# A macaron block on one core: router logits made with the router stationary, the first and last pass's gates spread by TensorE, small weights turned on chip, and every engine's order written anew

## The reference

```
x = x + 0.5 * ffn(layernorm(x))
x = x + attn(layernorm(x))          # 16 heads of 16, each token sees 64 keys back
x = x + 0.5 * ffn(layernorm(x))

ffn(X):  shared = silu(X @ sW1 + sb1) @ sW2 + sb2
         logits = X @ routing_W.T + expert_bias            # 8 experts
         g      = sqrt(softplus(logits)), only the two largest kept
         return shared + sum_e g[:, e] * (silu(X @ rW1[e] + rb1[e]) @ rW2[e] + rb2[e])
```

## Time and profile before

| what | value |
|---|---|
| median of three runs | 1589.93 us |
| profiled execution | 1584.86 us |
| its span | 1583.1 us |
| TensorE busy | 1479.5 us, 93% of the span |
| VectorE, ScalarE, GpSimd busy | 1179.6, 1128.6, 779.8 us |
| mean granted TensorE clock | 0.973 |

### The profile page before, as it was taken

One profiled execution on the slowest core, in us unless ns is written; L12 is line 12 of the kernel. 1 busy time (PEld: TensorE's weight loads), 2 busy tenths in 40 slices (PEclk: granted clock), 3 DMA queues, 4 the chain that ended last, 5 costly groups with the idle time before them and its releaser, 6 DMA issues.

```text
span 1583.1 us, 40702 instructions
## 1 busy us (share of the span) xinstructions
PE 1479.5 (93%) x13632; PEld 1333.7 (84%) x13632; DVE 1179.6 (75%) x4771; ACT 1128.6 (71%) x3400; POOL 779.8 (49%) x789
## 2 busy tenths in 40 slices
PE   2888999999999999999999999999999999998967
PEld 1777889898898989899898989989898988987756
DVE  5747677878878787887878787787878788675643
ACT  3358686877878687777878677787868778766823
POOL 2334454645555454555455455555546455453423
PEclk9899999999999999999999999999999999999888
DMA  4253635444453634445463543547364453625202
GB/s 116 64 164 106 174 111 177 121 125 137 122 172 95 192 110 138 129 124 161 121 181 102 155 128 116 157 124 180 95 176 121 126 138 107 173 82 161 82 20 67
DMA packets 269957, 203.86 MB, mean 129 GB/s; under 512 B 154379, under 2 KB 224421, under 8 KB 269749
## 3 DMA queue, kind: packets, MB, share of 16 engines
q1 hardware_dynamic: 266308, 201.17, 44.1%
q10 hardware_dynamic: 3408, 0.02, 0.1%
q0 software_dynamic: 32, 0.07, 0.0%
HBM read 146.06 MB, written 42.47 MB: 119 GB/s over the span
## 4 chain that ended last, share of the span: by engine, by line
PE 85%; DVE 5%; issue 3%; SPq 2%; DMA 2%; POOL 1%; ACT 1%; ACTq 0%; POOLq 0%; DVEq 0%
PE gb L937 12%; PE gb L939 11%; PE gb L938 11%; PE yb L937 9%; PE yb L939 8%; PE yb L938 8%; PE ptb L1000 7%; PE sb_ L991 6%; PE cxb L1019 4%; PE gb L1029 2%; PE gb L1041 2%; PE gb L1039 2%; PE gb L947 1%; SPq L479 1%; PE yb L1073 1%
## 5 line engine op out<-in xcount | busy, mean ns | idle before, releaser
L563 POOL TENSOR_TENSOR gl<-ag,gh 128x512 fp32r<-128x512 f32 x288 | 379.9, 1320 | 240.3 <-ACT gh L661 239.7
L546 POOL TENSOR_TENSOR pr<-pr,rinv 128x512 f32<-128x512 f32 x256 | 272.2, 1064 | 300.2 <-DVE rinv L822 298.3
L617 ACT ACTIVATE pr<-pr,mx 128x128 f32<-128x128 f32 x1024 | 397.5, 395 | 9.7 <-DVE mx L814 7.0
L937 PE MATMUL yb<-w2h,gh 128*128 128x256 f32 x1152 | 336.8, 292 | 12.4 <-POOL gl L563 12.3
L938 PE MATMUL yb<-w2h,gl 128*128 128x256 f32 x1152 | 324.0, 281 | 0.0
L939 PE MATMUL yb<-w2l,gh 128*128 128x256 f32 x1152 | 324.0, 281 | 0.0
L669 ACT ACTIVATE tt<-gb,b1half 128x512 f32<-128x512 f32 x288 | 195.4, 683 | 153.3 <-PE gb L939 147.7
L814 DVE CUSTOM_DVE_ANT_0 pr<-sb_,mask 128x128 f32<-128x128 f32 x1024 | 235.2, 285 | 53.8 <-issue 34.5
L881 DVE SCALAR_TENSOR_TENSOR ag<-gb,b,gate 128x512 f32<-128x512 f32 x256 | 188.2, 744 | 83.0 <-ACT tt L669 63.2
L661 ACT ACTIVATE gh<-ag 128x512 fp32r<-128x512 f32 x288 | 180.7, 628 | 95.1 <-DVE ag L887 66.8
L937 PE MATMUL gb<-xh,w1h 128*128 128x512 f32 x576 | 243.4, 423 | 2.6 <-DVE ag L881 2.0
(11 more groups left out here) (138 smaller groups left out, 2730.9 us busy)
## 6 DMA issues: line engine op xcount, KB each, us to landing
gate<-gates_pair SPq DMA_DIRECT2D x256, 256.0 KB, 3.7
ks<-qk_dram SPq DMA_DIRECT2D x256, 128.0 KB, 3.0
qs<-qk_dram SPq DMA_DIRECT2D x512, 64.0 KB, 2.6
qk_dram<-qkh SPq DMA_DIRECT2D x64, 256.0 KB, 2.4
qk_dram<-qkl SPq DMA_DIRECT2D x64, 256.0 KB, 2.7
vb<-va SPq DMA_DIRECT2D x32, 384.0 KB, 5.8
xres<-L_attn_x_dram SPq DMA_DIRECT2D x16, 512.0 KB, 4.1
out_dram<-xres SPq DMA_DIRECT2D x16, 512.0 KB, 4.0
```

Of the source, the lines that this page charges most:

```text
L546: nc.gpsimd.tensor_tensor(pr[:, k], pr[:, k], rinv[:, k, :].unsqueeze(2).to_broadcast([P, NP, P]), ALU.mult).then_inc(a_pn, 1)
L563: nc.gpsimd.tensor_tensor(gl[:, k, :], ag[:, k, :], gh[:, k, :].bitcast(F32), ALU.subtract).then_inc(f_gl, 1)
L617: nc.scalar.activation(pr[:, k, r, :], pr[:, k, r, :], ACT.Exp, bias=mx[:, k, r:r + 1], scale=-1.0, accum_out=rsum[:, k, r:r + 1]).then_in ...
L937: nc.tensor.matmul(dst, ah, bh, start=start, stop=False, **kw)
```

## The change

1. **Logits.** L now loads the router once for each half of the features (`rw`, widened with zeros to 128 columns) and streams `xh` and `xl`, 512 columns each: 4 matmuls. The result is turned: experts on partitions, rows 0 to 7 from the router's high part and rows 8 to 15 from its low part. A new ScalarE step lt copies the 128 by 512 tile to `lgt` in SBUF. A new TensorE step M takes each of its four 128-token parts as the stationary operand and a matrix `fold` of ones and zeros (8 columns) as the moving one, in true fp32, which turns the logits back and adds the two parts. Lr loses one of its two additions. The new value waits in the same bank, which is therefore held from L until Lr has read M's result.
2. **Gates of p0 and q15** (`by_pe`). They no longer go through DRAM. TensorE step B takes a column of the selection matrix `sel` as a broadcast stationary operand and streams `cft`: every partition gets the gate of one expert, in `sb_` or `ptb` in turn. ScalarE step K copies it to `gate`. So 16 matmuls of 512 columns and 16 copies are new, and two G1 and 16 sp are gone, as are two cr.
3. **Small weights.** The router and the biases were read transposed, element by element. Now their rows are read as they lie and TensorE step Wt turns them. GpSimd makes `sel`, `fold` and the zeros of `rw`.
4. **Loads** stand in the order of their use: x0, then 1s, 1r, 2s, 2r, then x1. The expert weights are split in halves (1r and 1t, 2r and 2t), so that their high and low parts are made in pieces. The zeroing Wz of `qs` and `va` moves from VectorE to GpSimd.
5. **All tables** are new. HEAD and TAIL of TensorE now reach further into the steady state, and ORDER, the steady period itself, is another sequence.

```diff
-P6-5 qC-6 S9-5 pY7-4 P7-5 S10-5 pY8-4 qH1-6 S11-5 qH2-6 U7-5 qY0-6 pX0-3 pX1-3 P8-5 qH3-6 P9-5 qY1-6 qH4-6
+aX0-2 qY1-4 aX1-2 qY2-4 S13-3 qH5-4 Q00-2 qY3-4 Q01-2 qY4-4 S14-3 pX0-1 pX1-1 qH6-4 S15-3 Q10-2 pL-1 P13-3
...
-pX0=0 pX1=0 pL=0 pH0=0 pC=0 pY0=0 pH1=0 pH2=0 pH3=0 pH4=0 pH5=0 pY1=0 pH6=0 pY2=0 pH7=0 pY3=0 pH8=0 pY4=0
+Wt=0 pX0=0 pX1=0 pL=0 pH0=0 pH1=0 pM=0 pH2=0 pC=0 pB0=0 pB1=0 pB2=0 pB3=0 pH3=0 pB4=0 pB5=0 pY0=0 pH4=0
...
-        rw = sb("rw", [P, KC, 2 * E], F32R)
-        rwf = sb("rwf", [P, KC, E])
+        rw = sb("rw", [P, KC, P], F32R)
+        fold = sb("fold", [P, E])
...
+        by_pe = {("p", 0), ("q", B - 1)}
...
+            apart_ |= {(x + k, b) for x, b in by_pe for k in ["G1", "cr"] + ["sp%d" % m for m in range(E)]}
...
-            for c in range(KC):
-                act.dma_start(rwf[:, c, :], routing_w[:, c * P:(c + 1) * P].rearrange("e p -> p e"),
-                              allow_slow_non_contiguous=True).then_inc(w_in[0], 16)
+            act.dma_start(small[0:E, 0:KC * P], routing_w).then_inc(w_small, 16)
+            act.dma_start(small[0:1, KC * P:], sb1.rearrange("(a p) -> a p", a=1)).then_inc(w_small, 16)
+            act.dma_start(small[1:NE, KC * P:], rb1).then_inc(w_small, 16)
...
+                elif s[1:] == "lt":
+                    n = nth(s, b)
+                    act.wait_ge(f_lgt, n + 1)
+                    nc.scalar.activation(lgt, bank(s[0] + "L", b), ACT.Copy).then_inc(f_lgs, 1)
...
+                elif s[1] == "K":
+                    n, m = nth(s, b), int(s[2])
+                    act.wait_ge(f_gpe, E * (s[0] == "q") + m + 1)
+                    wait(act, f_a, NE * (n - 1) + m + 6 if m < 4 else NE * n + m - 2)
+                    nc.scalar.activation(gate[:, m % 4, :], spread_to(m), ACT.Copy).then_inc(f_gk, 1)
...
+
+                    for k in range(KC):
+                        nc.tensor.matmul(tile, rw[:, k, :], xh[:, q, k, :], start=(k == 0), stop=False)
+                        mm = nc.tensor.matmul(tile, rw[:, k, :], xl[:, q, k, :], start=False, stop=(k == KC - 1))
+                    mm.then_inc(f_lgt, 1)
+                elif s[1] == "M":
+                    n = nth(s, b)
+                    pe.wait_ge(f_lgs, n + 1)
                     for t in range(NT):
...
+                        mm = nc.tensor.matmul(bank(s[0] + "L", b)[:, E * t:E * t + E], lgt[:, t * P:(t + 1) * P], fold[:],
+                                              start=True, stop=True, skip_group_check=True)
                     mm.then_inc(f_lg, 1)
...
+                    if m > 1:
+                        pe.wait_ge(f_gk, E * (s[0] == "q") + m - 1)
+                    nc.tensor.matmul(spread_to(m), sel[:, m:m + 1].to_broadcast([P, P]), cft[:], start=True, stop=True) \
+                        .then_inc(f_gpe, 1)
```

More of the change, by code:

```diff
@@ L85 @@
[L85 to L89, removed]
+pN1=0 Wl1s=0 Wlrw=0 pxl0=0 pxl1=0 Wl1r=0 pLr=0 pLq=0 pR1=0 Wl2r=0 Wl2s=0 pR2=0 pa0=0 Wl1t=0 pg0=0 pa1=0
@@ L171 @@
+qsp1=13 qsp2=13 qsp3=13 qsp4=13 qsp5=13 qsp6=13 qsp7=13 QW0=15 ST00=15 ST01=15 QW1=15 OUT=13 VS=15 ST10=15
+ST11=15 qG1=14 qsp0=14 qsp1=14 qsp2=14 qsp3=14 qsp4=14 qsp5=14 qsp6=14 qsp7=14 OUT=14 OUT=15
 """,
@@ L355, in split, with ns @@
             return pa[:, 2:4].rearrange("p w k n -> p (w k n)"), x1[1].rearrange("p t d -> p (t d)")
+        by_pe = {("p", 0), ("q", B - 1)}
+        def ns(s, b):
+            return sum(x not in by_pe for x in passes[:nth(s, b)])
         def wait(eng, s, value):
@@ L385, in heads, with spread_to @@
             return t[:, hd, 2 * u:2 * u + 2, :].rearrange("p b (a i d) -> p b a i d", i=2, d=DH)[:, :, :, hd, :]
+        def spread_to(m):
+            return sb_[:, :, :].rearrange("p r k -> p (r k)") if m % 2 == 0 else ptb[:]
         bank_no, bank_before = {}, {}
@@ L467, in step @@
                     c, hf = int(s[2]), int(s[3])
+                    if b == 0 and c == 0:
+                        sp.wait_ge(w_zero, 5)
                     if hf == 0:
@@ new lines, in _ @@
+            select(mask[0:WIN, 1, :], ALU.is_ge, NEG, -1, [[1, P]], -1)
+            select(mask[0:WIN, 1, :], ALU.is_ge, NEG, WIN, [[-1, P]], 1)
+            select(before[:], ALU.is_gt, 0.0, 0, [[1, E], [-1, E]], 0)
+            select(rowlo[:, 0:1], ALU.is_ge, 0.0, -48, [[0, 1]], 1)
+            select(rowlo[:, 0:1], ALU.is_ge, 0.0, 57, [[0, 1]], -1)
+            select(rowlo[:, 0:1], ALU.not_equal, 0.0, -56, [[0, 1]], 1)
+            select(sel32[:], ALU.not_equal, 1.0, -32, [[-1, E]], 1)
+            select(sel32[:], ALU.not_equal, 1.0, -40, [[-1, E]], 1)
@@ L537, in step @@
             def step(s, b):
-                if s == "rsa":
+                if s == "Wz":
+                    nc.gpsimd.memset(qs[:].bitcast(F32), 0.0).then_inc(w_zero, 1)
+                    pool.wait_ge(w_lo, max(lo_done("1r"), lo_done("1t")))
+                    nc.gpsimd.memset(va[:], 0.0).then_inc(w_zero, 1)
+                elif s == "rsa":
                     pool.wait_ge(a_stat, 8 * b + 8)
@@ L631, in step @@
                     act.wait_ge(f_rstd, 4 * n + 4)
-                    wait(act, f_g1, 16 * n)
+                    wait(act, f_g1, 16 * ns(s, b))
                     src = xin[b % NXI] if s[0] == "p" else x2
@@ L737, in ranks @@
             def ranks(n):
-                op = chain(n, 7)
+                op = chain(n, 6)
                 lj = lg[:].unsqueeze(2).to_broadcast([P, NT, E, E])
@@ L941, in step @@
             def step(s, b):
-                if s[:2] == "aX":
+                if s == "Wt":
+                    pe.wait_ge(w_small, 48)
+                    for c in range(KC):
+                        nc.tensor.transpose(turned[:, c * E:(c + 1) * E], small[0:E, c * P:(c + 1) * P], ident[0:E, 0:E])
+                    nc.tensor.transpose(turned[:, KC * E:KC * E + NE], small[:, KC * P:], ident[0:NE, 0:NE]) \
+                        .then_inc(w_smt, 1)
+                elif s[:2] == "aX":
                     c = int(s[2])
@@ L1063, in step @@
                     k = (NE * n + e) % NG
-                    weights("2s" if e == 0 else "2r", n == 0 and e < 2)
+                    weights("2s" if e == 0 else "2r" if e == 1 else "2t", n == 0 and e in (0, 1, 1 + E // 2))
                     pe.wait_ge(f_gl, NE * n + e + 1)
```

428 lines of the change are left out of this document (253 added, 175 removed).

## The result

The changed kernel takes 1615.15 us (median of 4 runs, 1612.63 to 1624.09) against 1590.16 for the kernel before: a ratio of 1.0168, interval 1.0128 to 1.0208. It is 25 us slower. The prediction was 1572 with a range up to 1595, so it was wrong in sign.

A forecast was written before the change was run, and what follows sets the result against it. TensorE, busy for 93% of the span, was taken as the bound. Start 7, rest of head 4, steady part 4 and tail 3 made 18 us off the profiled 1584.9, 1566.9; with the median 5.1 higher, 1572, range 1550 to 1595.

The forecast's parts named there:

- The steady order: Rewritten middle periods: same work but for L and M, 0.4 us less for each sequence, 5 us in all.
- the rivals: Three alternatives to 1572: larger gain, 1555, chance 0.20; slower by M's price, 0.15; time stays, 1587, 0.12.
- the one on the slower side: Rival: M's price on TensorE, 32 times, by four passes (1600) or lt late by 0.7 us; chance 0.15.
- M and L: Logits on TensorE: L 0.92 and M 0.88 us, together 1.80, 0.04 more than before, 1.3 us in 32 passes.
- lt was hidden: ScalarE's copy between L and M: about 1 us needed, covered by 1.7 to over 2 us of TensorE's other work.
- The start: First pass until Y1: X at 11.4, C at 35, Y1 near 46.5, 7 us earlier (bounds 4 to 10).
- Behind Y1: Experts of the first pass after Y1: both kernels bound by TensorE at about 2.8 us for an expert.
- The head: Run's beginning until OUT of sequence 0: 7 us from the start and 4 from the rest, OUT near 253.
- the 16.1 idle us between 60 and 150 us: TensorE's idle time in the rest of the head: a quarter expected back, 4 us (0 to 8).
- The tail: Last passes: new order gives 4 us, four B cost about 1; 3 us shorter (8 shorter to 4 longer).
- the sum: All terms: 7 + 4 + 4 + 3 = 18 us off the profiled 1584.9, giving 1566.9; median predicted 1572.

The follow-up runs named there:

- sp_before: Changed kernel with SyncE's middle list as before the change (VS behind OUT, G1, sp0 and sp1), all other engines keeping the new order: 1590.20 us, 1.0012.
- sp_all: Changed kernel with SyncE's middle list as before the change, and VS of sequences 2, 3, 4 and 14 behind psp1 in the ends: 1587.38 us, 0.9997.
- sp_all_old_logits: Changed kernel with SyncE's list put right in middle and ends, and the old logits (16 matmuls a pass, no lt, no M): 1594.51 us, 1.0033.
- before_early_x: Kernel before, with VectorE's statistics of x0 and x1 moved ahead of the step that waits for the element-wise bias load: 1586.56 us, 0.9988.

## Why the prediction was wrong, by its steps

- **The steady order, the step that failed and made the time wrong.** "It can win at most the 1.0 us of idle time for each sequence. I take 0.4": a cap on the gain and none on the loss. The work was the same, but I did not ask what each transfer waited for now stands behind. VS had moved on SyncE from behind sp1 to ahead of OUT and G1. In the kernel before the store landed at 723.8, 1.6 us ahead of aR0; behind VS it lands 3 us later (6.1 after its issue and not 3.0), and the new order of TensorE has O0 nearer to T, so that aR0 could come 4.4 us after T's start (sp_before) instead of 7.2. No cover was left. The twelve periods measured +3.1 us each, where -0.3 was forecast. Moving that one word back brings the time back to that of the kernel before (sp_before). None of the rivals was this; the one on the slower side was M's price.
- **M and L: the mechanism right, the price three times too small.** M has 8 records a pass. In sp_before L and M take 0.95 + 0.81 or 1.02 + 0.91 us, 1.76 to 1.93 together, against 1.70 to 1.76 for the old L (the starts of what follows, less their own): +0.12 a pass, about 4 us in 32 passes, where 1.3 were forecast. One of them, in sp_before:

```profile
564.80 0.48 PE L1161 MATMUL gb<-xh,rw 128*128 128x512 f32 x1
...
565.82 0.64 PE L1210 MATMUL yb<-b2s,cft 128*128 128x256 f32 x4
...
568.40 1.06 PE L1168 MATMUL gb<-fold,xn 128*128 128x8 f32 x8
569.31 0.36 PE L1054 MATMUL yb<-w2h,gh 128*128 128x256 f32 x1
```

lt was hidden: TensorE waited 0.7 us for it in the whole run of the changed kernel. The rule of the Trainium skill that true fp32 takes four passes (FP8 and Floating Point Precision, TensorE Precision Notes) would have made M 1.76; the runs show two records for each matmul and 0.81 to 0.91 for all eight.
- **The start: right in time until Y1, forecast 7, measured 9.1.** X at 12.12 (11.4 forecast), C at 31.83 (35), Y1 at 44.59 (46.5). VectorE's statistics of x0 began at 6.23 and not at 4.9: the cast of `sel` ahead of them waited for GpSimd's constants until 6.15, and so did TensorE's turn of the small weights.
- **Behind Y1: a second step that failed.** "After Y1 both kernels are bound by TensorE at about 2.8 us for an expert." The changed kernel was not. To the output bias of p0 it took 8.5 us before (53.70 to 62.16) and 13.8 now (44.59 to 58.35), with a mean granted clock of 0.88 instead of 1.00 and this wait in it:

```profile
49.55 0.50 PE L1054 MATMUL gb<-xh,w1h 128*128 128x512 f32 x1 [3.38 <-DVE ag L998]
...
58.35 0.64 PE L1210 MATMUL yb<-b2s,cft 128*128 128x256 f32 x4
```

VectorE came to that step a at 48.74, behind pieces of weight splitting, the output bias and the statistics of x1. Of the 9.1 us gained at Y1 3.8 were left.
- **The head: 11 forecast, 1.5 by its milestone, about 7 by its work.** OUT of sequence 0 came at 262.8, not near 253. T of sequence 0 started 4.0 us earlier than before; its store was issued 2.5 us after T's end, behind eight reads of Q on SyncE, and before at once:

```profile
263.06 1.29 DVE L898 SCALAR_TENSOR_TENSOR xres<-yb,xres 128x512 f32<-128x512 f32 x2 [0.49 <-PE yb L939]
```

```profile
259.01 1.29 DVE L1015 SCALAR_TENSOR_TENSOR xres<-yb,xres 128x512 f32<-128x512 f32 x2 [0.21 <-PE yb L1056]
```

By the new list TensorE also does V1, U13, U15 and C of the next passes ahead of that T instead of behind it, about 3 us by the lengths of such steps (an estimate). The parts agree with these 7: 3.8 left of the start, and 2.8 of the 16.1 idle us between 60 and 150 us gone, where 4 were forecast. The step of the prediction that the head lacks is the one behind Y1.
- **The tail: -4.8 us**, forecast -3, and near it in part by luck. U13 and U15 of sequence 13 are done ahead of it (about 1 us), and OUT of sequence 12 was issued 1.3 us after T's end, before 0.1; counted from T's start the tail is 3.5 shorter. From the last C to the first gated step 7.8 us passed (1578.75 to 1586.57), not 6.5, and before 6.6.
- **What the sum comes to without SyncE's mistake.** The profiled runs of sp_all and before have the same span (1583.0 and 1583.1): head -1.5, twelve periods +6.4, tail -4.9. Of the +6.4, L and M are about 2.9 by TensorE's records (1.2 by the periods of sp_all_old_logits), and 2.3 are the three long periods of the first part. What makes the rest is open, and it is more than the remainder of 1.2: V1 and C, some 1.8 us, have moved out of these periods into the head.

## What stays open

Whether the store's later landing comes from the bytes of VS in front of it, or in part from its own longer issue, no run tells apart. Nor was VS alone moved ahead in the kernel before. Open too is why the old logits in the corrected order, and the early X in the old order, come with falls of the clock between 60 and 264 us that sp_all does not have. The rows show that they do; no run turned such a fall on or off by itself. The new ends with the old middle order were not tried. No version beats the kernel before by what can be told; sp_all and before_early_x are level with it.

## What to carry to other kernels

Before trusting a reordered list, take each transfer that an engine waits for and read what now stands in front of it on its queue, in bytes as well as in issues; then set the margin between its landing and its use in the old trace against that: here it was 1.6 us, and two copies of 384 KB in front cost 3. When one wait is removed and the time stays, look for a second trip on the same queue that has taken its place before giving up the theory. An early start is worth what the slowest engine behind it can take up: follow every engine past the first wait that has gone. And a milestone in the middle of a rewritten order is only comparable after the work ahead of it is counted, and a store's issue is a milestone of its queue, not of TensorE.

## What the runs showed of the hardware

- **A transfer behind others on the same queue lands later, not only starts later.** The 512 KB store took 3.0 us to landing in the median when issued ahead of the two 384 KB copies (sp_before), 5.4 behind them; in the period shown the distance from T to its issue was the same. The Trainium skill (DMA: Bandwidth & Descriptors, Queues, rings and completion order) says that each DMA engine takes the descriptors of a ring in order; the two landing times agree with it. From the page of each, first the changed kernel:

```profile
out_dram<-xres SPq DMA_DIRECT2D x16, 512.0 KB, 5.4
```

```profile
out_dram<-xres SPq DMA_DIRECT2D x16, 512.0 KB, 3.0
```

- **A wait of 2.5 us of TensorE cost 1.8 us more.** Matmuls of 512 columns started every 0.43 us instead of 0.23 behind it, until 3.7 us after its end. Behind the wait of 1.9 us at 739.06 they did so too, from 740.18 on.
- **A faster start came with less clock later.** With X 6 us earlier in the old order the stretch from 20 to 60 us had clock 1.00 instead of 0.83, and the stretches from 60 to 150 had 0.87 instead of 0.91 and 0.94; that the one brought the other is not shown.
